# Key bias products behind the low parts, features in a place of their own, and four pieces of work put elsewhere

## The reference

```
x = x + decoder(layernorm(x), ctx)        # ctx: 8 x 722 x 512
  decoder: q, k, v = t @ in_proj.T + b ;  self attention ; out_proj ; norm 1 (g1, be1)
           q1 = x @ wq.T + bq ; k2 = ctx @ wk.T + bk ; v2 = ctx @ wv.T + bv
           cross attention ; norm 2 ; relu(x @ w1.T + b1) @ w2.T + b2 ; norm 3 (g3, be3)
x = x + ffn(layernorm(x))                 # 8 gates, top 2; experts share w1 (512 x 2048), w2
```

## Time and profile before

| | us |
|---|---|
| median of the runs | 524.13 |
| the profiled execution | 523.1 |
| its span, first to last instruction | 521.3 |
| TensorE busy | 510.3 |
| VectorE busy | 369.6 |
| ScalarE busy | 233.6 |
| GpSimd busy | 137.1 |

### The profile page before, as it was taken

One profiled execution on the slowest core, in us unless ns is written; L12 is line 12 of the kernel. 1 busy time (PEld: TensorE's weight loads), 2 busy tenths in 40 slices (PEclk: granted clock), 3 DMA queues, 4 the chain that ended last, 5 costly groups with the idle time before them and its releaser, 6 DMA issues.

```text
span 521.3 us, 7635 instructions
## 1 busy us (share of the span) xinstructions
PE 510.3 (98%) x2970; PEld 487.6 (94%) x2970; DVE 369.6 (71%) x630; ACT 233.6 (45%) x408; POOL 137.1 (26%) x112
## 2 busy tenths in 40 slices
PE   8899999999999999999999999999999999999997
PEld 7799999889988888999999999999999899999996
DVE  3753779886689896686579779468585387496645
ACT  2853542464588986255644334205525524151210
POOL 2430530014013124255504009005341531210000
PEclk9999999999999999999999999999999999999999
DMA  8951122031579962203702240201220022202004
GB/s 229 339 193 58 59 82 80 1 113 38 202 236 318 334 227 95 81 14 127 167 24 80 82 161 1 81 1 58 104 82 2 0 82 80 82 0 82 2 0 127
DMA packets 18444, 53.76 MB, mean 103 GB/s; under 512 B 1640, under 2 KB 2440, under 8 KB 15848
## 3 DMA queue, kind: packets, MB, share of 16 engines
q1 hardware_dynamic: 18348, 53.20, 31.0%
q10 hardware_dynamic: 60, 0.07, 0.1%
HBM read 51.63 MB, written 1.64 MB: 102 GB/s over the span
## 4 chain that ended last, share of the span: by engine, by line
PE 74%; DVE 14%; ACT 4%; DMA 3%; issue 3%; SPq 1%; POOL 0%; DVEq 0%; ACTq 0%
PE ps L693 15%; PE ps L695 15%; PE ps L694 15%; PE ps L738 3%; PE ps L737 3%; PE ps L736 3%; PE ps L792 3%; DMA WR<-wts_in 2%; PE ps L931 2%; PE ps L933 2%; PE ps L932 2%; PE ps L766 2%; DMA tok<-x_in 2%; PE ps L905 2%; PE ps L907 2%
## 5 line engine op out<-in xcount | busy, mean ns | idle before, releaser
L693 PE MATMUL ps<-AH,WH 128*128 128x400 f32 x284 | 98.8, 348 | 0.9 <-DVE AL L1432 0.7
L695 PE MATMUL ps<-AH,WL 128*128 128x400 f32 x284 | 98.0, 345 | 0.0
L694 PE MATMUL ps<-AL,WH 128*128 128x400 f32 x284 | 97.9, 345 | 0.0
L693 PE MATMUL ps<-XH,WH 128*128 128x400 f32 x224 | 78.5, 350 | 1.7 <-DVE acc L1453 0.9
L695 PE MATMUL ps<-XH,WL 128*128 128x400 f32 x224 | 77.3, 345 | 0.0
L694 PE MATMUL ps<-XL,WH 128*128 128x400 f32 x224 | 77.2, 345 | 0.0
L559 POOL TENSOR_TENSOR WL<-WR,WH 128x512 fp32r<-128x512 f32 x34 | 46.4, 1395 | 63.5 <-ACT WH L1089 63.5
L693 PEld LDWEIGHTS ps<-AH,WH 128*128 128x128 f32 x284 | 53.3, 188 | 2.5 <-DVE AL L1432 2.3
L694 PEld LDWEIGHTS ps<-AL,WH 128*128 128x128 f32 x284 | 53.4, 188 | 0.0
L695 PEld LDWEIGHTS ps<-AH,WL 128*128 128x128 f32 x284 | 53.4, 188 | 0.0
L693 PEld LDWEIGHTS ps<-XH,WH 128*128 128x128 f32 x224 | 42.1, 188 | 4.0 <-DVE acc L1453 1.2
(11 more groups left out here) (242 smaller groups left out, 1122.8 us busy)
## 6 DMA issues: line engine op xcount, KB each, us to landing
WR<-wts_in SPq DMA_DIRECT2D x19, 1024.0 KB, 4.8
ctR<-ctxt_in SPq DMA_DIRECT2D x16, 722.0 KB, 5.0
cnR<-ctxn_in SPq DMA_DIRECT2D x16, 512.0 KB, 5.0
cnR<-ctxn_in SPq DMA_DIRECT2D x8, 256.0 KB
tok<-x_in SPq DMA_DIRECT2D x4, 384.0 KB, 10.3
tok<-x_in SPq DMA_DIRECT2D x1, 1536.0 KB
cnR<-ctxn_in SPq DMA_DIRECT2D x8, 160.0 KB
VR<-wvo_in SPq DMA_DIRECT2D x4, 256.0 KB, 6.1
```

The lines of the kernel that those rows point to most:

```text
L693: pe.matmul(dst, wh, half(mh, h, k), start=(k == 0), stop=False)
L694: pe.matmul(dst, wh, half(ml, h, k), start=False, stop=False)
L695: mm = pe.matmul(dst, wl, half(mh, h, k), start=False, stop=(k == KC - 1))
```

## The change

It edits seven things:

1. The fp32 features of the first norm get tile XK in region R1 (over AH and AL of the second half) instead of XT in X. ScalarE waits for the first half's key sums before it evacuates the second half of U_A.
2. The key products leave `norm_features` and are placed later in VectorE's program: those of the first half between the splits of the first context tiles, those of the second between the evacuations of U_A's first half.
3. `self_normalise`: VectorE keeps the reciprocals; the four scalings go to ScalarE, after its first group of (U_K, 1) and after its first copies of attended values.
4. TensorE's third group of (U_CV, 1) is cut: three chunks, then the transposes to features, then its last chunk. VectorE's order of this stretch is as it was.
5. BLOCKS_AT: of the set U_F + 2, blocks 0 to 2 go from (U_F, 1) to the last group of (U_F + 1, 0), and 3 to 6 to one after each group of (U_F, 1).
6. GpSimd's last shift waits for the second group of (U_F + 6, 0) instead of the end of U_F + 4.
7. GpSimd's `inverse_deviation(7, 0)` goes ahead of `split_weights(U_M)`.

```diff
-BLOCKS_AT = {(U_F, 1): (U_F + 2, [[], [], [0, 1, 2], [3, 4]]), (U_F + 1, 1): (U_F + 2, [[5, 6], [], [], []]),
+BLOCKS_AT = {(U_F + 1, 0): (U_F + 2, [[], [], [], [0, 1, 2]]), (U_F, 1): (U_F + 2, [[3], [4], [5], [6]]),
...
-        XT = halves("XT", "X", F32, HS)
+        XK = [sb("XK%d" % h, "R1", 2 * HS + HS * h, [P, KC, HALF]) for h in range(2)]
...
-            pool.wait_ge(gemm_done, gemm_through(U_F + 4))
+            pool.wait_ge(gemm_done, gemm_count(U_F + 6, 0, 1))
             for b in range(B):
                 pool.tensor_tensor(tok[:, b, :], tok[:, b, :], be3b[0:T, :], ALU.add).then_inc(xres_ready, 1)
             inverse_deviation(6, 0)
+            inverse_deviation(7, 0)
             split_weights(U_M)
-            inverse_deviation(7, 0)
             split_weights(U_M + 1)
...
-            unit(U_CV, 1, [0, 1, 2])
+            unit(U_CV, 1, [0, 1])
+            unit(U_CV, 1, [2], range(KC - 1))
             to_features(2, 0, xn[0])
+            unit(U_CV, 1, [2], [KC - 1])
             unit(U_CV, 1, [3])
...
+            def self_normalise(h):                                   # ScalarE
+                act.wait_ge(s_rec, h + 1)
+                for j in range(HB):
+                    b = HB * h + j
+                    nm = act.activation(sprob[h][:, j, :], sprob[h][:, j, :], ACT.Copy, scale=srec[:, b:b + 1])
+                nm.then_inc(s_norm, 1)
...
-            unit(U_K, 1)
+            unit(U_K, 1, [0])
+            self_normalise(0)
+            unit(U_K, 1, [1, 2, 3])
             self_probT(0)
             self_exp(1)
             self_attended(0)
+            self_normalise(1)
             unit(U_VO, 0, [0, 1, 2])
...
             unit(U_A, 0)
+            act.wait_ge(key_ready, 1)
             unit(U_A, 1, [0])
...
-                settle(dve.reciprocal(srec[:, HB * h:HB * (h + 1)], ssum[:, HB * h:HB * (h + 1)]))
-                for j in range(HB):
-                    b = HB * h + j
-                    nm = dve.tensor_scalar(sprob[h][:, j, :], sprob[h][:, j, :], srec[:, b:b + 1], None, ALU.mult)
-                nm.then_inc(s_norm, 1)
+                dve.reciprocal(srec[:, HB * h:HB * (h + 1)], ssum[:, HB * h:HB * (h + 1)]).then_inc(s_rec, 1)
...
                     dve.wait_ge(x_high, 8 * i + KC * h + k + 1)
-                    if i == 1:
-                        key_product(h, k)
...
             split_cn(0, 0)
+            key_product(0, 0)
+            key_product(0, 1)
             normalise(1, 1, tiles[1])
             split_cn(0, 1)
+            key_product(0, 2)
+            key_product(0, 3)
             split_cn(0, 2)
...
-            unit(U_A, 0)
+            unit(U_A, 0, [0, 1])
+            key_product(1, 0)
+            key_product(1, 1)
+            unit(U_A, 0, [2])
+            key_product(1, 2)
+            unit(U_A, 0, [3])
+            key_product(1, 3)
             unit(U_A, 1, [0])
```

More of the change, by code:

```diff
@@ L657, in _, with unit @@
         def _(pe):
-            def unit(n, h, groups=range(KC)):
+            def unit(n, h, groups=range(KC), chunks=range(KC)):
                 at = POS[n, h]
@@ L685, in unit @@
                     dst = ps[:, bank(n, h, e), 0:HALF]
-                    for k in range(KC):
+                    for k in chunks:
                         if e == 0:
@@ L695, in unit @@
                         mm = pe.matmul(dst, wl, half(mh, h, k), start=False, stop=(k == KC - 1))
[L696 removed]
+                    if chunks[-1] == KC - 1:
+                        mm.then_inc(gemm_done, 1)
             def strassen(n):
@@ L1195, in norm_features @@
                     gain, shift = cst[:, gc + k:gc + k + 1], cst[:, bc + k:bc + k + 1]
-                    whole = XT if i == 1 else XF
+                    whole = XK if i == 1 else XF
                     if k % 2:
@@ L1587, in affine_features @@
                     dve.wait_ge(to_feat, 8 * i + KC * h + (KC if i == 2 else k + 1))
-                    dve.tensor_scalar(half(XT if i == 1 else XF, h, k), ps[:, 4 + k, 0:HALF], cst[:, gc + k:gc + k + 1],
+                    dve.tensor_scalar(half(XK if i == 1 else XF, h, k), ps[:, 4 + k, 0:HALF], cst[:, gc + k:gc + k + 1],
                                       cst[:, bc + k:bc + k + 1], ALU.mult, ALU.add).then_inc(x_affine, 1)
@@ L1593, in norm_features @@
                     dve.wait_ge(x_high, 8 * i + KC * h + k + 1)
-                    if i == 1:
-                        key_product(h, k)
-                    src = (half(XT if i == 1 else XF, h, k) if i in (1, 2) else
+                    src = (half(XK if i == 1 else XF, h, k) if i in (1, 2) else
                            ps[:, k if (i, h) == (0, 0) else 4 + k, 0:HALF])
@@ L1611, in key_product @@
                         dve.wait_ge(gv_ready, 1)
-                    dve.tensor_scalar(keyX[h][:, :], half(XT, h, 0), key, qks[:, 0:1], ALU.mult,
+                    dve.tensor_scalar(keyX[h][:, :], half(XK, h, 0), key, qks[:, 0:1], ALU.mult,
                                       ALU.add).then_inc(key_step, 1)
@@ L1615, in key_product @@
                 dve.wait_ge(key_step, (KC - 1) * h + k)
-                dve.scalar_tensor_tensor(out=keyX[h][:, :], in0=half(XT, h, k), scalar=key, in1=keyX[h][:, :],
+                dve.scalar_tensor_tensor(out=keyX[h][:, :], in0=half(XK, h, k), scalar=key, in1=keyX[h][:, :],
                                          op0=ALU.mult, op1=ALU.add
```

1 line of the change is left out of this document (added).

## The result

The changed kernel took 530.23 us (median of 4 runs, 529.7 to 531.61) and the kernel before 523.87 beside it (4 runs). The ratio is 1.0136, interval 1.012 to 1.0152, which is 7.1 us slower (6.3 to 8.0); the two medians lie 6.4 us apart and the spans of the two profiles 6.6. The profiled execution took 529.7, its span 527.9, the mean granted clock was 0.997; in the other three executions it was 0.994. TensorE has the same work (511.6 us busy against the earlier trace rows) and waits longer.

A forecast was written before the change was run, and what follows sets the result against it. TensorE, busy 98% of the span, was taken as the bound, so only later starts count. Terms -0.7 - 1.15 + 1.2 + 0.7 + 0.8 + 1.4 - 1.05 + 3.3 + 1.9 = +6.4 on 523.6 gave 530.0 us, range 525.0 to 532.4.

The forecast's parts named there:

- Scalings on ScalarE: Self attention: four scalings leave VectorE, so TensorE's stop before 81.63 goes; -0.7 us, bounds -0.7 to 0.
- Key products out of the lows: First half's lows: three key products leave the chain ahead of the last evacuation; -1.15 us, bounds -1.3 to -0.6.
- The first half's products ahead of the A product: Two products fall in VectorE's wait, two delay the A product's start; +1.2 us, bounds 0 to 1.7.
- The second half's products in U_A: Stop before 121.55 goes (-0.7), a 1.4 stop appears at the cross scores; net +0.7 us.
- Transposes ahead of the last chunk: Cut group of (U_CV, 1): completes later, delaying the affine features and first XL; +0.8 us, bounds -0.45 to +1.3.
- Blocks beside the feature sums: Fifth weight set: block lows take turns with GpSimd's feature sums, making relu lows late; +1.4 us, bounds -0.4 to +2.2.
- The last shift later: GpSimd's eight additions start later, so the stop before 325.45 goes; -1.05 us, bounds -1.17 to -0.2.
- The power ahead of the weights' lows: First FFN-2 weights: later lows delay the next load; M product +3.3 us, following down product +1.9 us.
- Wrong: the M product starting without a wait: Sign against the forecast, which had the M product start some 3 us late with ScalarE waiting for the load.
- no turns: Rival: VectorE's moved operations miss GpSimd's, so the sum is +1.6 us, 525.2 us; chance 0.13.
- The moves only shift waits: Rival: stops reappear in the same size and the late load costs half; +2.6 us, 526.2 us; chance 0.08.
- Port held through the power: Rival: the power holds the shared port, a key product ends 0.6 us later; sum 7.0, 530.6 us; chance 0.09.

The follow-up runs named there:

- experiment 10: Kernel before with only the scalings on ScalarE and GpSimd's last shift later: 522.04 us, ratio 0.9972.
- experiment 9: Kernel before with only the blocks of set U_F + 2 moved earlier (BLOCKS_AT): 524.83 us (one run) against 524.12.
- experiment 1: Changed kernel with the power again behind the four weight lows of U_M: 524.73 us, ratio 1.001.
- experiment 2: Kernel before with only the power put ahead of split_weights(U_M): 529.75 us, ratio 1.0107.
- experiment 5: Changed kernel with GpSimd waiting after each of U_M's four weight lows for that low's own semaphore: 530.43 us, ratio 1.0141.
- experiment 6: Changed kernel with one GpSimd wait for the power's end before the four weight lows of U_M: 529.72 us, ratio 1.0122.
- experiment 7: Kernel before with only the features in XK and the key products moved: 523.81 us, ratio 0.9996.
- experiment 3: Changed kernel with a GpSimd wait before U_M's lows that named a unit long over, so held nothing back: 531.48 us, ratio 1.0137.
- experiment 4: Changed kernel with GpSimd's four U_M lows held until VectorE made the fourth relu low of (U_M - 2, 1): 531.39 us, ratio 1.0141.

## Why the prediction was right, and where it was not

The forecast was 530.0 and the measured time 530.23. The sum was +6.4; the medians give +6.4, the spans +6.6 and the ratio +7.1.

- *Scalings on ScalarE*, -0.7: the stop (0.61 and a restart) is gone, here and in experiment 10. Right. Four scalings took 1.19 us on ScalarE, inside the bound of 1.7.
- *Key products out of the lows*, -1.15: the 1.21 are gone. Right.
- *The first half's products ahead of the A product*, +1.2: 1.48 lost instead of 0.30, +1.2. Right.
- *The second half's products in U_A*, +0.7: the old 0.59 went, the new stop lost 0.90. Net +0.3: the term was too large. From the start of the A product the fourth low ended 12.0 us on (12.3 forecast) and TensorE arrived 11.2 us on (11.0 forecast): two small errors of one sign.
- *Transposes ahead of the last chunk*, +0.8: 1.06 instead of 0.35, and the restart of the cut group; about +0.8. Right.
- *Blocks beside the feature sums*, +1.4: 0.51 + 0.37 + 0.44 + 0.45 - 0.62 + 0.3 for three more restarts = +1.45. Right, by turns as said, and shown alone in experiment 9.
- *The last shift later*, -1.05: the 1.07 and its restart went, and the stop at 334 grew by 0.21: -0.97. Right.
- *The power ahead of the weights' lows*, +3.3 and +1.9: edit 7 cost 5.5 to 6.6 (experiment 1) or 5.6 (experiment 2) where the two make 5.2. The size is about right, but this is the step that failed. The forecast had the four lows "taking turns with VectorE's low" and the loss at the M product. In the changed kernel there were no turns: the relu low was shut out for all four, TensorE lost 4.65 us there, 0.37 before, and 1.5 more at half clock, for which the sum had no term. That is 5.8 in all. The late load came as forecast, 4.97 us behind the last low where 4.89 were counted, and found TensorE already later than itself. Experiments 5 and 6 let the turns be taken and show the forecast's chain with about its sizes: 0.98 - 0.37 + 0.24 + 2.91 + 0.23 + 1.28 = 5.3 and the restarts. So two costs of nearly one size lie over each other and only the larger shows. That the total came out right is in part luck, and it alone could not have told which of the two was at work.
- "Wrong: the M product starting without a wait", the prediction said of itself. It did.

Of the rivals, *no turns* had VectorE's moved operations miss GpSimd's; three of the second half's four key products, the three blocks and the relu lows met them. *The moves only shift waits* has a share: experiment 7 shows it for the key products. *Port held through the power* was set aside on the earlier trace rows, and rightly: the second product in the wait for the deviation, which by that rule was to end 0.6 us later, began 0.27 us into the power and took 0.63. The held low is not it either: that one began when the power was over. But a hold longer than one operation did exist, in the lows behind the power.

Not foreseen: stops of 0.35 and 0.55 in the cross attention. They stand before products with ptL, in other places and sizes in each profile (0.2 to 0.9), also in kernels that don't touch this stretch; the kernel before has one of 0.25. And the first products, up to 23 us, went 0.9 us faster than in the kernel before. I take both for the varying times of loads; no run tested that.

## What to carry to other kernels

Before work is moved on GpSimd, follow the buffer that its last instruction frees to the next load, and that load to the engine that copies it: here a power of 1.0 us, put ahead of four lows, made the next load some 5 us later. When a removed stop does not shorten the time, look for the same microseconds at the next reader; a piece of work on VectorE is only free in a gap of VectorE where GpSimd is quiet too (0.6 us a product there, 1.1 to 1.6 beside GpSimd). Price each edit alone: two of the seven won 1.5 us (0.8 to 2.1; 1.8 by the medians) and the other five hid it.

## What the runs showed of the hardware

**A low was shut out by four GpSimd operations in a row.** Elsewhere VectorE's two-operand work beside GpSimd's large operations ends one operation later: 1.66 instead of 0.62 in the earlier trace rows, 2.29 instead of 0.58 beside the feature sums. Beside the small power it did not wait at all (0.57 in the earlier trace rows, 0.63 at 103.75). Behind the power, with the first weight low begun 0.03 us before the power's end and the other three ready, it waited for all four: 4.93 us in three of three profiles (the change, experiments 2 and 3). With a wait behind the power, or behind each low, it took 1.37 and 1.27, in one profile each. Being ready in a row is not enough, as experiment 6 shows. The eight additions of the last shift run without waits between them, and a relu low of the changed kernel, begun at 331.80 beside one that ended at 332.74, had ended by 333.18. Why the sequence behind the power differs is not settled.

The Trainium skill (SBUF — State Buffer, "Who interferes with whom") says that a VectorE instruction with two SBUF inputs contends with a GpSimd instruction that reads SBUF, and that whoever issues first has the shared ports for the whole instruction. The turns of this case agree with it (1.55 and 1.12 for a product of 0.62). The operations begun inside a power do not (0.57 and 0.63, no longer than alone). The 4.93 go beyond it: the rule is for one instruction, and here it was four.

**The granted clock fell with the long stops.** After stops drawn as 4.48, 4.48 and 4.37 us idle (the change, experiments 2 and 4) the clock was 0.50 to 0.57 in the 4 us shown above, against 1.00 before them: the lower of the two levels, 1.2 instead of 2.4 GHz, and matmuls stood 0.33 apart. What it cost was not the same each time: some 1.5 us in the change, 2.1 in experiment 2 (where it was down from about 364, in the middle of the stop, to 371) and 2.9 in experiment 4 (down from about 376 to 383). After 2.75 us idle (the profile of experiment 5) it stayed at 1.00. So in these profiles one stop of some 4.6 us cost 6.2 to 7.4, and nearly 5 us in four pieces, as in experiment 6 (mean clock 1.000 and 0.999 in its two executions), cost only themselves.
